# Attention with a top-2 expert layer: one stack of transfers held back four scores, the rows of maxima and two token transposes two units earlier

## The reference

```
xs = layernorm_over_channels(x).reshape(B, T, C)            # B=16, T=1024, C=128
q, k, v = per-head projections of xs                        # 8 heads of 16
out = softmax(q k^T / 4) v, per head; out @ Wproj + bproj
x1 = x + out
t = tokens of x1;  n = layernorm(t)
gates = softmax(n @ w_gating)                               # 16 experts
top-2 experts of each token, capacity 256 per image and expert
y = combine(relu(expert_inputs @ w1) @ w2)                  # 128 -> 512 -> 128
output = t + y
```

## Time and profile before

| | |
|---|---|
| median of 3 runs | 2619.81 us (2619.79 to 2620.16) |
| the profiled execution | 2619.64 us |
| its span, first to last instruction | 2617.6 us |
| TensorE busy | 88% |
| VectorE busy | 74% |
| ScalarE busy | 58% |
| GpSimd busy | 45% |

### The profile page before, as it was taken

One profiled execution on the slowest core, in us unless ns is written; L12 is line 12 of the kernel. 1 busy time (PEld: TensorE's weight loads), 2 busy tenths in 40 slices (PEclk: granted clock), 3 DMA queues, 4 the chain that ended last, 5 costly groups with the idle time before them and its releaser, 6 DMA issues. The chain is left out here.

```text
span 2617.6 us, 59768 instructions
## 1 busy us (share of the span) xinstructions
PE 2308.6 (88%) x14610; PEld 1154.0 (44%) x14610; DVE 1937.4 (74%) x4671; ACT 1508.5 (58%) x2881; POOL 1185.6 (45%) x1833
## 2 busy tenths in 40 slices
PE   3999999999999999989999999999819999999963
PEld 1223333332333333333333323333219999999952
DVE  6888888888888888878888888888425555555544
ACT  0576676767666676757667676676604444444420
POOL 5214446373553637264463725444354444444420
PEclk9999999999999999999999999999959999999985
DMA  2233322224322222423222233222062222222249
GB/s 45 34 45 53 62 42 58 33 58 59 65 50 42 58 33 60 60 49 63 42 58 33 58 58 62 55 34 50 19 186 65 64 63 62 63 64 63 62 126 282
DMA packets 142489, 166.33 MB, mean 64 GB/s; under 512 B 25214, under 2 KB 97284, under 8 KB 142370
## 3 DMA queue, kind: packets, MB, share of 16 engines
q1 hardware_dynamic: 125474, 131.08, 25.1%
q0 software_dynamic: 16896, 34.12, 4.7%
HBM read 60.66 MB, written 44.67 MB: 40 GB/s over the span
## 5 line engine op out<-in xcount | busy, mean ns | idle before, releaser
L842 DVE TENSOR_REDUCE sb_m_red<-banks 128x1 f32<-128x512 f32 x2048 | 1339.1, 680 | 256.4 <-PE banks L1264 244.5
L705 ACT ACTIVATE sb_arena_a<-banks 128x512 f32<-128x512 f32 x2048 | 1142.8, 599 | 518.5 <-PE banks L1286 471.6
L1286 PE MATMUL banks<-sb_arena_b 104*128 104x512 bf16 x2048 | 700.6, 383 | 33.6 <-DMA sb_arena_b<-sb_m_row 31.6
L1264 PE MATMUL banks<-sb_arena_b 96*128 96x512 bf16 x2048 | 690.1, 388 | 38.9 <-DMA sb_arena_b<-sb_arena_c 25.2
L1303 PE MATMUL banks<-sb_arena_a,sb_arena_d 128*32 128x512 f32 x4096 | 546.2, 605 | 9.6 <-ACT sb_arena_a L705 8.7
L1286 PEld LDWEIGHTS banks<-sb_arena_b 104*128 104x128 bf16 x2048 | 198.1, 97 | 492.3 <-ACT sb_arena_a L705 337.3
L688 POOL DMA_INDIRECT expert_out<-sb_arena_d x272 | 267.4, 983 | 306.2 <-DVE sb_arena_d L1168 265.2
L1264 PEld LDWEIGHTS banks<-sb_arena_b 96*128 96x128 bf16 x2048 | 199.7, 98 | 403.2 <-DVE sb_m_red L842 272.7
L1439 PE MATMUL banks<-sb_arena_d,sb_arena_c 128*128 128x128 f32 x2176 | 291.2, 277 | 40.5 <-ACT sb_arena_d L813 40.5
L633 POOL DMA_INDIRECT sorted_rows<-sb_rows,sb_place x256 | 248.0, 969 | 98.5 <-issue 91.2
L820 ACT ACTIVATE sb_arena_c<-banks 128x512 f32<-128x512 f32 x272 | 162.4, 597 | 219.9 <-PE banks L1439 219.9
(11 more groups left out here) (145 smaller groups left out, 1803.4 us busy)
## 6 DMA issues: line engine op xcount, KB each, us to landing
sb_arena_b<-sb_arena_c SPq DMA_DIRECT2D x384, 128.0 KB, 5.4
sb_arena_d<-sorted_rows SPq DMA_DIRECT2D x272, 66.0 KB, 1.8
sb_arena_a<-expert_out SPq DMA_DIRECT2D x32, 512.0 KB, 5.6
sb_x_in<-in_x_dram SPq DMA_DIRECT2D x16, 512.0 KB, 3.4
sb_res<-in_x_dram SPq DMA_DIRECT2D x16, 512.0 KB, 7.6
sb_x_all<-sb_res SPq DMA_DIRECT2D x16, 512.0 KB
out_dram<-sb_arena_a SPq DMA_DIRECT2D x16, 512.0 KB, 3.9
expert_out<-sb_arena_d POOLq DMA_INDIRECT x272, 2.2
```

Source lines behind the costliest of these rows:

```text
L705: nc.scalar.activation(probs[:, u % PRING, :], ps_score[:, u % RING, :], ACT.Exp, scale=SCALE).then_inc(exp_done, 1)
L842: nc.vector.tensor_reduce(out=m_red[:, s % 2, u:u + 1], in_=ps_max[:, m % SLOTS % RING, :], axis=AX.X, op=ALU.max).then_inc(max_taken, 1)
L1264: nc.tensor.matmul(ps_max[:, m % SLOTS % RING, :], qs[0:STACK, g, h, half * HALF + t * P:half * HALF + (t + 1) * P], ks[0:STACK, g, h, kh ...
L1286: nc.tensor.matmul(ps_score[:, u % RING, :], ks[0:STACK + MROWS, g, h, i * P:(i + 1) * P], qs[0:STACK + MROWS, g, h, half * HALF:(half + 1 ...
```

## The change

Three things, all in the order of the first stage. The row of maxima is made at unit 24 of each segment and copied at unit 25, in place of 26 and 27. The two token transposes are at units 20 and 22, in place of 22 and 24, and their copies at 21 and 23. The transfers of group 1, from the second image on, wait for the first four scores of their own image besides all scores of the image before. Nothing is added or removed, and every instruction keeps its size.

```diff
-MSLOT = 26
+MSLOT = 24
...
-            def stack(b, g):
+            def stack(b, g, late=0):
-                wait_apart(sp, sp_passed, scores_ready, SLOTS * (b - 1) + 2 * UNITS * (g + 1))
+                wait_apart(sp, sp_passed, scores_ready, SLOTS * (b - 1) + (2 * UNITS if g == 0 else SLOTS + late))
...
-                stack(b, 1)
+                stack(b, 1, 0 if first else 4)
...
+                        if u == 21:
+                            copy_tokens(b - 1, 0)
                         if u == 23:
-                            copy_tokens(b - 1, 0)
-                        if u == 25:
                             copy_tokens(b - 1, 1)
...
+                        if u == 20:
+                            transpose_tokens(b - 1, 0)
                         if u == 22:
-                            transpose_tokens(b - 1, 0)
-                        if u == 24:
                             transpose_tokens(b - 1, 1)
```

## The result

The changed kernel takes 2628.1 us, the median of 8 runs (2621.6 to 2632.6), against 2619.9 for the kernel before (8 runs, 2617.1 to 2621.6). The ratio is 1.0028, with a 95% interval of 1.0019 to 1.0038: slower by 0.28%. The forecast of 2622.5 us meant no change that can be told; the result lies inside its range, on the side that had 0.28. The profiled execution took 2626.24 us.

The account below looks back on a forecast made before the run. TensorE paces units 29 to 63 and 82 to 107, group 0's transfer chain 63 to 82, GpSimd 107 to 29. Terms +1.5, +1.0, -0.2, +0.5 sum to +2.8 us: 2622.5 us, range 2616 to 2630.

Parts of the forecast that it names:

- The step that failed: Unit 64: removing the wait for the row of maxima gains nothing, as TensorE then waits 1.7 us at unit 82.
- the zero for the token transposes: Units 20 to 24: moved token transposes cost zero, all before unit 29 under GpSimd; without that cover 0.2 us.
- Cost zero in this image: Group 1 held back: new 2.2 us wait at unit 18, covered by 2.51 us TensorE had to spare at unit 29.
- the one of the long stop: Rival: GpSimd's one 8.1 us wait falls elsewhere; gone 2615 us, twice 2630 us; chance 0.04.
- Unit 96: Removing the wait for the row of maxima there gains 0.6 us an image, bounds 0.45 and 0.76.
- Unit 56: New wait for ScalarE's copy of v costs 0.7 us in 15 images, bounds 0.6 and 0.78.
- The rival of a free wait there: Rival: the new wait at unit 56 costs nothing because VectorE is full there, 2612 us; chance 0.1.
- Unit 18: New wait of 2.2 us for group 1's transfers, issued at 873.2 and landed at 888.0.
- the +0.5 for it: Allowance of 0.5 us in all for images where the wait for GpSimd at unit 29 covers too little.
- The last image: Sum of -0.2 us: 1.0 uncovered at unit 18, less 0.6 at unit 96 and 0.6 at unit 64.
- The late landing: Rival: scatters slow group 1's transfers beyond GpSimd's cover at unit 18; 2628.5 us, or 2631; chance 0.25.
- All of the 31.6 us come back: Rival: every wait for the row of maxima in the first stage is regained, 2588 us; chance 0.03.

Follow-up runs that it names:

- The filler behind unit 81: The changed kernel plus four 128x512 products with unused results behind unit 81, inside the wait at unit 82: 2620.3 us, ratio 0.9999.
- the one early row: The kernel before with the row of maxima two units earlier only in the third segment (unit 88 in place of 90): 2606.8 us, ratio 0.9946.
- without the two parts that cost: The changed kernel with the second segment's row of maxima back at unit 58 and group 1 transfers not held back: 2603.5 us, ratio 0.9940.
- group 1 not held back: The changed kernel with its group 1 transfers no longer held back, rows of maxima and token transposes as changed: 2623.7 us, ratio 1.0012.
- group 1 alone: The kernel before with only its group 1 transfers held back four scores, from the second image on: 2637.0 us, ratio 1.0068.
- tokens alone: The kernel before with only the token transposes moved to units 20 and 22, and their copies to 21 and 23: 2629.4 us, ratio 1.0045.
- group 0 later with filler: The kernel before with group 0 transfers waiting for one more score, plus eight products with unused results behind unit 81: 2645.6 us, ratio 1.0086.
- group 0 later: The kernel before with group 0 transfers waiting for one more score (65 in place of 64), from the second image on: 2656.1 us, ratio 1.0136.

## Why the prediction was near in its time and wrong in its mechanism

**The step that failed** is that TensorE "only reaches unit 82 sooner and waits 1.7 us there in place of 1.09", as "nothing". The wait came out at 1.71 us, as said. What was wrong is that a longer wait under a chain costs nothing: the chain ends when it did, but TensorE then does the next products at half clock, in 4 of 15 images, 1.4 us each. The filler behind unit 81 is the test: the same landing, the same reach of unit 82, only less idle time, and the half clock is gone there, and with it 7.8 us of the median. The same idea stands behind the zero for the token transposes, because "All of it lies before unit 29, under GpSimd": alone they cost 9.6 us, and a filler brings these back. It stands also behind "Cost zero in this image" for group 1, whose wait of 2.0 us, alone, was followed by half clock 10 times in 15. In the changed kernel these two weren't put to the test in an ordinary image: its waits there are 1.4 us at unit 18 and 0.5 at unit 29, and none of them lost the clock. Of the rivals only the one of the long stop named the clock, 0.69 around the 8.1 us; none had it fall behind a short wait.

**The terms of the sum.**

- Unit 96: I took 0.6, with 0.76 as the upper bound. It measured 0.87 in an ordinary image in three kernels. The bound counted the 0.55 and the 0.21 of the earlier trace rows as listed. But a wait costs somewhat more than its listed idle time: scores 95 and 96 started 1.37 us apart in that image, and 0.66 where the wait is gone, so the 0.55 listed was 0.71 of delay. That term was some 4 us too small over the first 15 images.
- Unit 56: I took 0.7, and above 0.78. It measured 0.79. The 0.61 us that the profile lists are again less than the delay. The rival of a free wait there is dead.
- Unit 18: I said 2.2 us, and it was 1.37 (0.87 to 1.44 in 12 images). TensorE came to unit 18 13.96 us behind score 3 (877.49 to 892.82 - 1.37), not 13.27 as in the earlier trace rows; 0.48 of the 0.69 us more are a new wait for VectorE at unit 3. The group landed 15.33 us behind score 3, where I had 15.5. So in these images the cover was never short, and the +0.5 for it wasn't needed. The reason I gave for it was misread: the 20.3 us in 13 waits hold one of 5.4 us at the very start, and the twelve at unit 29 are 0.88 to 1.40 us, 1.24 in the mean, and not 1.56. In the second and the last image, where I had counted +1.0 each, the waits were 2.3 and 2.7 us and the stretches 2.8 and 2.2 us longer; half clock stood behind the second image's.
- The last image: of the two times 0.6 us that I took off, neither came. Unit 29 to 107 takes 60.14 us before and after. TensorE reached unit 64 0.94 us sooner and then waited 0.96 us for one of VectorE's reductions; what is gained at 96 only makes up for the further waits of this kind.
- The new order of the tokens and the rows of maxima at units 20 to 24 went as said: the 0.6 us moved to L1273.

Five stretches of half clock are new, four behind unit 82 and one behind unit 18 of the second image. The table's sums add up to +6.2 us, and 5 x 1.4 = 7.0 of it are these five. At full clock, the rest left as it is, that sum would be -0.8. A shorter long stop of GpSimd (-3.8 us, below), which I hadn't in the sum either, is part of it.

**Luck.** That the time lies within the range is in part luck. The clock (+7.0 us) and the last image (+2.2 in place of -0.2) were left out or missed on one side, the long stop (-3.8) and the size of the gain at unit 96 (some -4) on the other. The range did not foresee any of the four as they came.

**The rivals.** The late landing didn't come: group 1 was issued at 878.14 and unit 18 went on at 892.82, 14.7 us for transfers wholly beside scatters, against group 0's 14.8 without. The rule of taking turns, which I had set beside it from the Trainium skill, "DMA: Bandwidth & Descriptors", section on queues, rings and completion order, made no difference that could be seen in the landing. The time was near this rival's 2628.5 for another reason. "All of the 31.6 us come back" fell as argued: two thirds of the waits stood under other chains, and the one early row gained nearly all there was.

**What would show it.** No waits at 0, 64 and 96; L1273 once an image for v; the wait at 82 near 1.7; the x wait down to about 0.5, where I had said 0.3: all there. The wait at unit 18 was to be near 2.2 and was 1.37. "An image's length as before within 0.3 us" held for an image with full clock (113.4 us in place of 113.5), and not for those without. I had listed waits and lengths as signs, and not the granted clock of the stretches behind the waits.

## What to carry to other kernels

A wait that lies under another engine's chain can be free at its present length and cost when it grows. If an edit makes TensorE arrive sooner there, or joins two short waits to one, read the granted clock of the stretch behind it, and try a few products with an unused result in the idle time: here 4 or 5 an image gave back 8 us. Before moving a step at all places at once, cut the loop into stretches by what ends them and move it only in the stretch that TensorE paces, and not behind a copy that frees the same bank; one early row of four was worth more than the whole change.

## What was unexpected of the hardware

**The clock after waits of one and a half to three microseconds.** Each line is TensorE's idle time ahead of one unit and how often its granted clock was at half behind it, in one profiled execution each:

| kernel and place | idle us | half clock |
|---|---|---|
| before, unit 82 | 0.89 to 1.48 | 0 of 15 |
| before, unit 29 | 0.88 to 1.40 | 0 of 12 |
| without the two parts that cost, unit 29 | 1.44 to 1.83 | 0 of 12 |
| changed, unit 82 | 1.41 to 2.20 | 4 of 15 |
| group 1 not held back, unit 29 | 1.42 to 1.96 | 2 of 12 |
| group 1 alone, unit 18 | 1.80 to 2.80 | 10 of 15 |
| tokens alone, unit 29 | 2.19 to 2.75 | 6 of 12 |
| changed, unit 18, 13 images | 0.87 to 1.44 | 0 of 13 |
| changed, unit 18, second and last | 2.31, 2.66 | 1 of 2 |
| group 0 later with filler, unit 29 | 1.04 to 1.66 | 2 of 12 |
| group 0 later, unit 82 | 2.15 to 2.90 | 13 of 15 |

On the whole it falls more often the longer the idle time is, but the rows don't follow in order, and the length alone doesn't decide. In the changed kernel at unit 82, 2.20 us kept the clock at 268.63 and 1.69 us lost it at 610.46:

```profile
268.63 0.39 PE L1264 MATMUL banks<-sb_arena_b 96*128 96x512 bf16 x1 [2.20 <-DMA sb_arena_b<-sb_arena_c]
...
610.46 0.39 PE L1264 MATMUL banks<-sb_arena_b 96*128 96x512 bf16 x1 [1.69 <-DMA sb_arena_b<-sb_arena_c]
```

The shortest wait with half clock behind it was 1.48 us, at unit 29 of group 0 later with the filler. What tells such waits apart stays open; no run here tried it.

The runs of one kernel differ in it too. Of the changed kernel's 8 runs the fastest (2621.6 us) had a mean granted clock of 0.966 and the slowest (2632.6) 0.962; with the tokens alone it was 0.964 at 2624.5 us and 0.959 at 2635.0. The kernel before isn't free of it either: of its 15 runs on one chip the slowest, 2627.2 us, had 0.964, where the fastest, 2619.0, had 0.968. A kernel that loses the clock nearly every time doesn't spread for that: group 0 later, 2.9 us over 4 runs.

**GpSimd's long stop.** In one image of each run, the same one in all kernels, GpSimd stands still for microseconds ahead of one of its scatters. GpSimd in order of time at that place, first in the kernel before, then in the changed one:

```profile
1107.44 0.96 POOL L633 DMA_INDIRECT sorted_rows<-sb_rows,sb_place  x1 [6.97 <-issue]
```

```profile
1109.77 0.96 POOL L633 DMA_INDIRECT sorted_rows<-sb_rows,sb_place  x1 [3.16 <-issue]
```

It was 6.9 to 7.1 us in the eight kernels that issue group 1 at its old place, and 3.2 to 3.8 in the four that hold it back. So holding group 1 back goes with a stop that is some 3.8 us shorter in the changed kernel, and that is part of why the changed kernel isn't slower still. A second stop, in the scatters behind the last image's unit 127, is 3.2 to 3.4 us in all twelve kernels. What these stops are, and why a transfer of another queue shortens one of them, was not tried and stays open.
